# Second-layer expert dispatch: a table of slots and a gather per tile, or whole rows scattered into expert order; and the order of the start-up loads

## The chip, the cores and the metric

The kernel runs on one core of one Trainium2 chip. The metric is device time in microseconds (us) of one execution. Only the device time counts; the transposes of weights and context that the launch code makes on the host are outside it, and the change leaves them as they are.

## The reference

Two layers follow each other on x of 32 batches x 100 tokens x 256 (3200 tokens). Each layer is a cross-attention on a context of 361 rows x 192 per batch, then a mixture of experts:

```python
x = x + tanh(g_xattn[0]) * L0_xattn(layernorm(x), ctx, ...)      # 8 heads of 64
x = x + tanh(g_ffn[0])   * L0_ffn(layernorm(x), ...)             # 8 experts, top 2, hidden 512
x = x + tanh(g_xattn[1]) * L1_xattn(ctx, layernorm(x), mask, ...) # 4 heads, masked, rms-normed q and k
x = x + tanh(g_ffn[1])   * L1_ffn(layernorm(x), ...)             # 16 experts, top 4 of 2 groups, hidden 256

# L1_ffn, per expert e (we is the token's weight for e, 0 if not chosen)
h = silu(x2 @ W1[e].T + b1[e]) * (x2 @ W3[e].T + b3[e])
y = y + (h @ W2[e].T + b2[e]) * we[:, None]
```

Four of sixteen experts for each of 3200 tokens are 12,800 rows in the second expert layer.

## The kernel before

`build` (line 61) runs five stages one after the other, each a block in which the five engines have their own instruction lists and meet at a barrier at its end: `setup` (141), `attention0` (270), `experts` for layer 0 (1379), `attention1` (782), `experts` for layer 1.

**setup.** GpSimd (POOL) makes constants. SyncE's queue (SP) issues all small and middle weights of both layers, ten small vectors first, then the key and value weights of layer 0, then the others (185 to 202), and all of them are waited for (203, 212, 234). ScalarE's queue (ACT) fills two slot tables in DRAM with "empty" entries and zeroes spare rows (228 to 233). attention0 begins when all of it has landed.

**Attention, both layers.** One iteration of a software pipeline works on one batch in several phases at once: `i` is the batch whose scores are made, `i+1` to `i+4` are batches whose inputs are loaded, normalised and projected, `i-1` and `i-2` are routed. In layer 1, per iteration, SP loads x (859) and context and mask (868 to 870; line 866 waits until POOL has used the mask of two batches before), and stores x1 and the normalised rows xm (877, 879). VectorE (DVE) begins with the context's statistics (1133), which wait for that load; then come the norms, the route (1207 to 1256) and the dispatch (1263 to 1274). POOL does the roots (1312, 1336), the softmax's normalising (1349), the mask (1328), and four indirect DMAs (1357). `y_dispatch` gives each token and choice a position: the count of the expert's tokens so far, in that expert's region of the table. Each of the four DMAs of a batch writes 100 entries of 8 bytes (token number, weight) to table1 at these positions; the normalised rows go to xn1 in token order by the plain store 879.

**Experts.** The tiles have 128 rows each: 57 tiles for layer 0 and 115 for layer 1, some of them empty at the end. First DVE turns the counts into a plan (1481 to 1501): for each tile its expert (`tile_e`), its first table row (`tile_r`) and whether it is the first of its expert (`tile_s`). TensorE (PE) turns the plan into rows (1687 to 1689). Layer 1 meanwhile loads the biases, copied to all partitions (1607 to 1609, 2 MB each); DVE's first tile waits for them. Then for each tile j: SP loads 128 table entries (1570), POOL gathers the 128 rows of xn that they name (1438), PE transposes (1634), ACT copies (1583), PE multiplies by W1 and W3 (1652), DVE adds the bias (1526), ACT takes SiLU (1594), DVE multiplies (1531), PE transposes (1668), ACT copies (1600), PE multiplies by W2 (1680), DVE adds the bias (1540) and multiplies by the entry's weight (1545), POOL adds the rows to the output in DRAM by an indirect DMA (1451). POOL's list is written out: gather j+3, then scatter j-2. A scatter waits for the scatter two before it, and, where its tile is the first of an expert, for the one before it.

```python
for j in range(NT):
    gather(j + LOOK)          # xg<-xn,slots  L1438
    if j >= 2:
        scatter(j - 2)        # out<-y,slots  L1451
```

PE's list for one tile is x_transpose(j+1), down(j-2), h_transpose(j-1), up(j+1).

Of the kernel before, what the change touches and what calls it, by code (L numbers as in the profile page):

```python
# [7 lines left out]
F32 = mybir.dt.float32  # L8
# [23 lines left out]
REGION = TOKENS  # L32
# [28 lines left out]
def build(nc, a, out):  # L61
    top = ExitStack()
    dram = {}
    for n, e, t in ((0, E0, NT0), (1, E1, NT1)):
        rows = e * REGION + (t + 3) * P
        dram[f"table{n}"] = nc.dram_tensor(f"table{n}", (rows, 2), I32, kind="Internal").ap()
        dram[f"xn{n}"] = nc.dram_tensor(f"xn{n}", (TOKENS + SPARE, D), F32, kind="Internal").ap()
# [15 lines left out]
    with top:  # L83
# [12 lines left out]
            experts0_loaded=sem("experts0_loaded"), experts1_loaded=sem("experts1_loaded"),  # L96
        )
        c["wk0"] = c["expert_w"][:, 0:2 * I0].rearrange("p (k n) -> p k n", k=2)
        c["wv0"] = c["expert_w"][:, 2 * I0:4 * I0].rearrange("p (k n) -> p k n", k=2)
        first = ExitStack()  # L100
# [8 lines left out]
        experts(nc, maker, a, dram, c, 1)  # L109
# [11 lines left out]
W0_LOADS, W1_LOADS = 2 * E0, 3 * E1  # L121

# [17 lines left out]

def setup(nc, maker, a, dram, c):
    stack = ExitStack()
    with stack:
        sb, ps, sem = maker(stack)
        empty = sb("empty_slots", [P, SPARE, 2], I32)
        zero = sb("zero_rows", [P, D])
        odd, even = sb("odd", [P, 1], I32), sb("even", [P, 1], I32)
        ones_set, tables_set = sem("ones_set"), sem("tables_set")
        w_loaded, filled = sem("w_loaded"), sem("filled")
        halved, gates_done, scale_done = sem("halved"), sem("gates_done"), sem("scale_done")  # L150
        tall = (("wk0", "L0_xattn_Wk"), ("wv0", "L0_xattn_Wv"))
        small = (("wq0", "L0_xattn_Wq", P), ("wo0", "L0_xattn_Wo", P), ("wr0", "L0_ffn_moe_router", P),
                 ("wq1", "L1_xattn_WqT", P), ("wkv1", "L1_xattn_WkvT", CK), ("wlkv1", "L1_xattn_WlkvT", P),
                 ("wo1", "L1_xattn_WoT", P), ("wr1", "L1_ffn_WgT", P))
        W_LOADS = 6 + 4 + 3 * len(tall) + len(small) + 2
        FILLS = 0
        for n in range(2):
            FILLS += -(-(dram[f"table{n}"].shape[0] // SPARE) // P) + 4
        with nc.Block() as block:

            @block.gpsimd
            def _(g):
                g.memset(c["ident"][:, :], 0.0)
                g.memset(empty[:, :, :], 0)
                g.memset(zero[:, :], 0.0)
                g.memset(c["upto"][:, :, :], 1.0)
                g.memset(c["ones"][:, :], 1.0).then_inc(ones_set, 1)
                g.wait_ge(ones_set, 1)
# [3 lines left out]
                                base=0, pattern=[[1, N]], channel_multiplier=-1)  # L172
                g.affine_select(out=c["upto"][:, :, :], in_=c["upto"][:, :, :], compare_op=ALU.is_ge, fill=0.0,
# [5 lines left out]
                g.iota(c["token"][:, :], [[1, 1]], base=0, channel_multiplier=1)  # L179
                g.iota(empty[:, :, 0], [[1, SPARE]], base=TOKENS, channel_multiplier=0).then_inc(tables_set, 1)  # L180

            @block.sync
            def _(s):
                with nc.allow_non_contiguous_dma(reason="a few per-partition constants"):
                    s.dma_start(c["gates"][:, 0:2], a["g_xattn"].partition_broadcast(P)).then_inc(w_loaded, 16)
                    s.dma_start(c["gates"][:, 2:4], a["g_ffn"].partition_broadcast(P)).then_inc(w_loaded, 16)
                    s.dma_start(c["cx_g"][:, :], a["L1_xattn_ln_x_g"].rearrange("(k p) -> p k", p=CK)).then_inc(w_loaded, 16)
                    s.dma_start(c["cx_b"][:, :], a["L1_xattn_ln_x_b"].rearrange("(k p) -> p k", p=CK)).then_inc(w_loaded, 16)
                    s.dma_start(c["lt_g"][:, :], a["L1_xattn_ln_l_g"].rearrange("(k p) -> p k", p=P)).then_inc(w_loaded, 16)
                    s.dma_start(c["lt_b"][:, :], a["L1_xattn_ln_l_b"].rearrange("(k p) -> p k", p=P)).then_inc(w_loaded, 16)  # L190
                    for half in range(2):
                        r = slice(half * DH, (half + 1) * DH)
                        s.dma_start(c["qk_g"][r, 0:1], a["L1_xattn_qn_g"].rearrange("(p k) -> p k", k=1)).then_inc(w_loaded, 16)
                        s.dma_start(c["qk_g"][r, 1:2], a["L1_xattn_kn_g"].rearrange("(p k) -> p k", k=1)).then_inc(w_loaded, 16)
                for n, src in tall:
                    s.dma_start(c[n][:, 0, :], a[src][0:P]).then_inc(w_loaded, 16)
                    s.dma_start(c[n][0:CR, 1, :], a[src][P:C]).then_inc(w_loaded, 16)
                    s.dma_start(c[n][P - CR:P, 1, :], a[src][P:C]).then_inc(w_loaded, 16)
                for n, src, p in small:
                    s.dma_start(c[n][:, :, :], a[src].rearrange("(k p) n -> p k n", p=p)).then_inc(w_loaded, 16)  # L200
                s.dma_start(c["bo0"][:, :], a["L0_xattn_bo"].partition_broadcast(N)).then_inc(w_loaded, 16)
                s.dma_start(c["bo1"][:, :], a["L1_xattn_bo"].partition_broadcast(N)).then_inc(w_loaded, 16)
                s.wait_ge(w_loaded, 16 * W_LOADS)

            @block.vector
            def _(v):
                v.memset(c["neghalf"][:, :], -0.5)
                v.wait_ge(tables_set, 1)
                v.tensor_scalar(even[:, :], odd[:, :], 1, 4, ALU.arith_shift_right, ALU.logical_shift_left).then_inc(halved, 1)
                v.wait_ge(halved, 1)  # L210
                v.tensor_scalar(c["landed"][:, :], even[:, :], float(-16 * (P // 2)), None, ALU.add)
                v.wait_ge(w_loaded, 16 * W_LOADS)
                v.tensor_tensor(c["qk_s"][:, :], c["qk_g"][:, 0:1], c["qk_g"][:, 1:2], ALU.mult).then_inc(scale_done, 1)
                v.wait_ge(scale_done, 1)
                v.tensor_scalar(c["qk_s"][:, :], c["qk_s"][:, :], DH ** -0.5, None, ALU.mult)
                v.wait_ge(gates_done, 1)
                v.tensor_scalar(c["bo0"][:, :], c["bo0"][:, :], c["tg"][0:N, 0:1], None, ALU.mult)
                v.tensor_scalar(c["bo1"][:, :], c["bo1"][:, :], c["tg"][0:N, 1:2], None, ALU.mult)

            @block.scalar  # L220
            def _(s):
                s.wait_ge(tables_set, 1)
                for n in range(2):
                    t = dram[f"table{n}"]
                    assert t.shape[0] % SPARE == 0
                    blocks = t.shape[0] // SPARE
                    full = t.rearrange("(b r) c -> b (r c)", r=SPARE)
                    for at in range(0, blocks, P):
                        m = min(P, blocks - at)
                        s.dma_start(full[at:at + m], empty[0:m].rearrange("p r c -> p (r c)")).then_inc(filled, 16)  # L230
                    for at in range(TOKENS, TOKENS + SPARE, P):
                        s.dma_start(dram[f"xn{n}"][at:at + P], zero[:, :]).then_inc(filled, 16)
                        s.dma_start(dram[f"acc{n}"][at:at + P], zero[:, :]).then_inc(filled, 16)
                s.wait_ge(w_loaded, 16 * W_LOADS)
                s.activation(c["tg"][:, :], c["gates"][:, :], ACT.Tanh).then_inc(gates_done, 1)
                s.wait_ge(filled, 16 * FILLS)
# [33 lines left out]
def attention0(nc, maker, a, dram, c):  # L270
# [8 lines left out]
    with stack:  # L279
# [21 lines left out]
        x1_out, xm_out, slots_out = sem("x1_out0"), sem("xm_out0"), sem("slots_out0")  # L301
        ready, w_high, w_low = sem("ready0"), sem("w_high"), sem("w_low")
        ln_dve, ln_pool, xb_done = sem("ln_dve0"), sem("ln_pool0"), sem("xb_done0")
# [16 lines left out]
        with nc.Block() as block:  # L320

            @block.sync
            def _(s):
# [17 lines left out]
                def store(b):  # L341
                    if b >= 1:
                        s.wait_ge(x1_out, 16 * b)
                        s.wait_ge(xm_out, 16 * b)
                    s.wait_ge(x1_done, b + 1)
                    s.dma_start(acc_b[b], r["x1"][:, b % 2, :]).then_inc(x1_out, 16)
                    s.wait_ge(ln1_dve, nth(LN, b, "done"))
                    s.dma_start(xn_b[b], r["xm"][:, b % 2, :]).then_inc(xm_out, 16)

                s.wait_ge(ready, 1)  # L350
                for b in range(3):
                    load_x(b)
                    load_c(b)
                for b in range(B):
# [6 lines left out]
                    if b == B - 4:  # L361
                        load_experts0(s, a, c)
                store(B - 1)
                s.wait_ge(x1_out, 16 * B)
                s.wait_ge(xm_out, 16 * B)

            @block.tensor
# [1377 lines left out]
```

## Time and profile before

| | us |
|---|---|
| median of 3 runs (2165.41 to 2174.96) | 2169.73 |
| the profiled execution, own time | 2168.25 |
| its span, first to last instruction | 2166.5 |
| PE busy | 1943.0 (90%) |
| DVE busy | 1341.7 (62%) |
| POOL busy | 1272.2 (59%) |
| ACT busy | 926.0 (43%) |

The stages lie in the span about so: setup 0 to 26, attention0 26 to 740, experts of layer 0 740 to 1080, attention1 1090 to 1729, experts of layer 1 1729 to 2166. A timeline row has start, duration, engine, line, operation, written tile and read tiles, and in brackets how long the engine was idle before it and what ended that. A group row has count, busy time in all and mean ns of one, then the idle time before its instructions.

### The profile page before, as it was taken

The numbers are of one execution on the slowest core, as the hardware profiler recorded it, in microseconds if no ns is written. First come the engines' busy times: TensorE is split into PE (matmuls) and PEld (weight loads), VectorE is DVE, ScalarE is ACT, GpSimd is POOL, SyncE is SP. The second block draws the span as 40 slices with busy tenths as digits, with TensorE's granted clock in tenths as the row PEclk, the third lists the DMA queues.
The fourth block names the chain that finished last, engine by engine and source line by source line (L and its number), as shares of the span: only waits on it lengthen the run. The fifth ranks groups of instructions, "written<-read, shape, count | busy, mean of one in ns | idle before, by whom it ended". The sixth has DMA issues, their size and how long they took to land. (4 is left out here: it accounts for less than half of the span.)

```text
span 2166.5 us, 40335 instructions
## 1 busy us (share of the span) xinstructions
PE 1943.0 (90%) x11418; PEld 1339.4 (62%) x11418; DVE 1341.7 (62%) x4049; ACT 926.0 (43%) x2321; POOL 1272.2 (59%) x1490
## 2 busy tenths in 40 slices
PE   3999999999999289999679999999999469899997
PEld 2777777777777168888535555555555335555554
DVE  3677777777776532222348888888888435555554
ACT  1444443444433323333147666666776123333332
POOL 1344444444444344545347888888888347777776
PEclk9999999999999689999879999999999589999999
DMA  4111101011116023333211111111117154445454
GB/s 130 35 28 37 39 27 39 26 39 37 28 57 223 10 40 53 51 54 50 42 35 36 36 36 36 36 36 35 36 35 236 40 146 76 76 75 79 74 77 73
DMA packets 143799, 127.49 MB, mean 59 GB/s; under 512 B 48505, under 2 KB 134241, under 8 KB 143590
## 3 DMA queue, kind: packets, MB, share of 16 engines
q0 software_dynamic: 39456, 46.11, 13.2%
q1 hardware_dynamic: 96348, 70.67, 11.7%
q10 hardware_dynamic: 7786, 8.14, 1.1%
q8 instruction: 105, 1.72, 0.4%
q14 instruction: 104, 0.85, 0.1%
HBM read 87.16 MB, written 37.65 MB: 58 GB/s over the span
## 5 line engine op out<-in xcount | busy, mean ns | idle before, releaser
L747 POOL TENSOR_SCALAR prob<-prob,rc 100x363 f32<-100x363 f32 x256 | 158.2, 627 | 343.3 <-DVE rc L610 343.3
L1680 PE MATMUL psD<-expert_w,hT 128*128 x916 | 232.7, 387 | 3.0 <-ACT hT L1600 3.0
L1438 POOL DMA_INDIRECT xg<-xn,slots x178 | 178.9, 1005 | 91.9 <-issue 46.9
L1451 POOL DMA_INDIRECT out<-y,slots x115 | 186.5, 1621 | 75.2 <-issue 28.4
L1652 PE MATMUL psG<-expert_w,xgT 128*128 x460 | 219.7, 600 | 1.3 <-ACT xgT L1583 1.3
L937 PE MATMUL psJ<-wkv,cTn 96*121 96x512 f32 x384 | 177.7, 600 | 0.0
L1680 PEld LDWEIGHTS psD<-expert_w,hT 128*128 128x128 f32 x916 | 161.5, 191 | 21.6 <-issue 5.0
L1451 POOL DMA_INDIRECT acc<-y,slots x57 | 89.7, 1573 | 137.2 <-DVE y L1545 132.3
L536 ACT ACTIVATE prob<-psS,nm 100x361 f32<-100x361 f32 x256 | 141.5, 561 | 54.0 <-DVE nm L605 50.9
L605 DVE TENSOR_REDUCE nm<-psS 100x2 f32<-100x722 f32 x128 | 115.0, 898 | 71.6 <-PE psS L434 71.4
L1357 POOL DMA_INDIRECT table<-slot,pos x128 | 137.7, 1076 | 35.6 <-issue 30.1
L1583 ACT ACTIVATE xgT<-psX 128x256 f32<-128x256 f32 x115 | 44.1, 383 | 256.1 <-PE psX L1634 256.1
L1522 DVE TENSOR_TENSOR hid<-psU,gate 128x512 f32<-128x512 f32 x57 | 39.4, 691 | 159.1 <-PE psU L1642 159.1
L1634 PEld LDWEIGHTS psX<-ident,xg 128*128 128x128 f32 x344 | 41.6, 142 | 151.8 <-DMA xg<-xn,slots 104.2
L1600 ACT ACTIVATE hT<-psH 128x256 f32<-128x256 f32 (+1 forms) x172 | 77.8, 452 | 129.6 <-PE psH L1668 127.3
L1336 POOL TENSOR_TENSOR rk<-rk,neghalf 121x12 f32<-121x12 f32 x64 | 126.9, 1982 | 5.3
L1526 DVE TENSOR_TENSOR pre<-psG,bias 128x512 f32<-128x512 f32 x115 | 79.5, 691 | 76.1 <-PE psG L1652 68.8
L614 DVE COPY pT<-psT 121x600 f32<-121x600 f32 x128 | 99.1, 774 | 42.8 <-PE psT L442 42.7
L1634 PE MATMUL psX<-ident,xg 128*128 128x128 f32 x344 | 71.0, 288 | 60.7 <-DMA xg<-xn,slots 45.3
L541 ACT ACTIVATE oT<-psO 128x100 f32<-128x100 f32 x128 | 32.4, 253 | 206.4 <-PE psO L455 202.7
L1060 ACT ACTIVATE kv<-psJ 121x512 f32<-121x512 f32 (+2 forms) x160 | 88.0, 550 | 69.7 <-PE psJ L937 69.7
L1652 PEld LDWEIGHTS psG<-expert_w,xgT 128*128 128x128 f32 x460 | 79.7, 194 | 58.3 <-issue 58.3
(271 smaller groups left out, 5049.6 us busy)
## 6 DMA issues: line engine op xcount, KB each, us to landing
expert_w<-in_L_ffn_moe_w SPq DMA_DIRECT2D x8, 1024.0 KB, 13.6
xn<-xm SPq DMA_DIRECT2D x64, 100.0 KB
bias<-in_L_ffn_b ACTq DMA_DIRECT2D x3, 2048.0 KB, 13.8
ctx<-in_ctx SPq DMA_DIRECT2D x32, 181.5 KB
cT<-in_ctxT SPq DMA_DIRECT2D x32, 180.5 KB
cT<-in_ctxT SPq DMA_DIRECT2D x64, 90.2 KB
expert_w<-in_L_ffn_moe_w SPq DMA_DIRECT2D x8, 512.0 KB, 12.3
expert_w<-in_L_ffn_W1T SPq DMA_DIRECT2D x16, 256.0 KB
```

Source lines behind the costliest of these rows:

```text
L536: s.activation(prob[:, q, 0:S], psS[0:N, h, 0:S], ACT.Exp, bias=nm[:, q:q + 1], accum_out=rs[:, q:q + 1]).then_inc(exp_done, 1)
L605: v.tensor_reduce(nm[:, q2:q2 + 2], psS[0:N, :, 0:S], AX, ALU.max, negate=True).then_inc(max_done, 1)
L614: v.tensor_copy(pT[:, p % 2, :, :, :], psT[0:CH, :, 0:NCH * N].rearrange("p h (j n) -> p h j n", j=NCH)).then_inc(t_out, 1)
L747: g.tensor_scalar(prob[:, q, :], prob[:, q, :], rc[:, q:q + 1], 1.0, ALU.mult, ALU.mult).then_inc(prob_done, 1)
L937: mm = t.matmul(ph[0:rows, 0:cols], lhs, wt[:, k, :], start=k == 0, stop=k == 1)
L1336: g.tensor_tensor(rk[:, b % 3, lo:hi, :], rk[:, b % 3, lo:hi, :], neghalf[0:CH, 0:1].unsqueeze(2).to_broadcast([CH, hi - lo, H1]), ALU.pow ...
L1357: g.indirect_dma_start(table, bass.IndirectOffsetOnAxis(r["pos"][:, b % 2, k:k + 1], 0), r["slot"][:, b % 2, k, :], None).then_inc(slots_o ...
L1438: g.indirect_dma_start(xg[:, j % 4, :], None, xn_rows, bass.IndirectOffsetOnAxis(slots[:, j % RING, 0:1].bitcast(U32), 0)).then_inc(gather ...
L1451: g.indirect_dma_start(acc, bass.IndirectOffsetOnAxis(slots[:, j % RING, 0:1].bitcast(U32), 0), y[:, j % 4, :], None, compute_op=ALU.add). ...
L1634: mm = t.transpose(psX[:, k * P:(k + 1) * P], xg[:, j % 4, k * P:(k + 1) * P], ident[:, :])
L1652: mm = t.matmul(psG[:, r, :], xT[:, r, k, :], w13[:, bass.ds(e, 1), k, 0:512], start=k == 0, stop=k == 1)
L1680: mm = t.matmul(psD[:, r, 0:D], hT[:, r, k, :], w2[:, bass.ds(e, 1), k, :], start=k == 0, stop=k == KF - 1)
```

## The change

It touches the start of the kernel and the second layer's way from attention to experts.

- **Start.** setup no longer waits for weights: SP loads only the key and value weights of layer 0, ACT the six other loads that attention0 needs; the fills and the 14 loads for attention1 are issued by SP within attention0, between the inputs of batch 1 and those of batch 2. Waits for each group stand where it is first used: TensorE and ACT for layer 0's weights, POOL's first slot scatter for the fills, DVE at iteration 8 for layer 1's weights.
- **Row scatter.** table1 and xn1 are gone. attention1 keeps for each token one row of 273 floats (256 normalised values, the token number, the 16 expert weights, zero where not chosen) and scatters the whole row (1092 bytes) four times, to the position in each chosen expert's region of `rows1`. The store of xm is gone. DVE's wait for these scatters moves from the dispatch to the norm and looks two batches further back.
- **Plan.** The 18 small DVE steps, the PE rows and the three copies stand at the end of attention1's lists. SP and ACT each end 8 regions with 128 empty rows (DRAM to DRAM, 16 copies of 140 KB) once the counts are known; the stage ends when they have landed.
- **Experts of layer 1** are a function of their own: SP loads tile j's 128 rows with one plain DMA into a ring of 8; there is no table load and no gather, POOL only scatters. The weight is a column of the row, picked by the tile's expert number.

```diff
-REGION = TOKENS
+REGION = TOKENS + P
+ROW = D + 1 + 16
...
+            @block.sync        # setup
+                for n, src in (("wk0", "L0_xattn_Wk"), ("wv0", "L0_xattn_Wv")):
+                    s.dma_start(c[n][:, 0, :], a[src][0:P]).then_inc(c["kv0_loaded"], 16)
...
-                s.wait_ge(w_loaded, 16 * W_LOADS)
...
                 # attention0, sync
-                s.wait_ge(ready, 1)
-                for b in range(3):
+                for b in range(2):
                     load_x(b)
+                    if b == 0:
+                        s.wait_ge(ready, 1)
                     load_c(b)
+                fill(s, dram, c)
+                load_attention1(nc, s, a, c)
+                load_x(2)
+                load_c(2)
...
                 # attention1, sync, store(b)
-                    s.dma_start(acc_b[b], r["x1"][:, b % 2, :]).then_inc(x1_out, 16)
-                    s.wait_ge(ln1_dve, nth(LN, b, "done"))
-                    s.dma_start(xn_b[b], r["xm"][:, b % 2, :]).then_inc(xm_out, 16)
+                    s.dma_start(acc_b[b], r["x1"][:, b % 2, :]).then_inc(stored, 16)
...
                 # attention1, vector
                 def y_norm(b):
+                    if b >= 4:
+                        v.wait_ge(slots_out[b % 2], 64 * (b // 2 - 1))
-                    v.tensor_scalar(r["xm"][:, b % 2, :], r["x1"][:, b % 2, :], ...
+                    v.tensor_scalar(row[:, b % 4, 0:D], r["x1"][:, b % 2, :], ...
                 def route_weights(b):
-                    n = rt.inc(v.tensor_scalar(w, top_v[:, 0:TOP1], tmp[:, 1:2], ROUTE_SCALE, ALU.mult, ALU.mult))
+                    n = rt.inc(v.scalar_tensor_tensor(w, r["sc"][:, 0, :], tmp[:, 1:2], r["chosen"][:, :], ALU.mult, ALU.mult))
...
                 # attention1, gpsimd, scatter(b, k)
-                    g.indirect_dma_start(table, bass.IndirectOffsetOnAxis(r["pos"][:, b % 2, k:k + 1], 0),
-                                         r["slot"][:, b % 2, k, :], None).then_inc(slots_out[b % 2], 16)
+                    g.indirect_dma_start(rows, bass.IndirectOffsetOnAxis(pos[:, b % 4, k:k + 1], 0),
+                                         row[:, b % 4, :], None).then_inc(slots_out[b % 2], 16)
...
+        def empty_tails(engine, which):
+            for e in which:
+                end = engine.value_load(base_i[0:1, e:e + 1], ...)
+                engine.dma_start(rows[bass.ds(end, P), :], rows[E1 * REGION:E1 * REGION + P, :]).then_inc(emptied, 16)
...
+def experts1(nc, maker, a, dram, c):
+            @block.sync
+                for j in range(NT):
+                    if j >= RING:      # RING = 8
+                        s.wait_ge(scattered[j % 2], 16 * ((j - RING) // 2 + 1))
+                    if j >= 4:
+                        s.wait_ge(rows_in[j % 4], 16 * (j // 4))
+                    at_row = s.value_load(tile_r[0:1, j:j + 1], ...)
+                    s.dma_start(xr[:, j % RING, :], rows[bass.ds(at_row, P), :]).then_inc(rows_in[j % 4], 16)
+            @block.gpsimd
+                for j in range(NT):
+                    scatter(j)
+            @block.vector      # weighted(j)
+                    v.tensor_scalar(y[:, j % 4, :], yb[:, j % 2, :], row_w[:, j % RING, bass.ds(e, 1)], None, ALU.mult)
```

The lists of TensorE, ACT and the rest of DVE in experts1 are those of layer 1 before.

## Rows read from the trace of the kernel before

**Rows 1.** Windows: the tiles of experts layer 1, and attention1; busy us (instructions) by engine, clock, DMA share, GB/s

```profile
1754.20:2153.40 399.20, 366.32 (x1360) 208.96 (x1360) 217.37 (x453) 130.72 (x342) 290.74 (x223) 0.99 0.48 74
1154.00:1690.00 536.00, 519.57 (x3158) 312.62 (x3157) 440.38 (x1732) 365.33 (x810) 454.31 (x570) 0.99 0.20 57
```

**Rows 2.** Groups by line and shape, and waits, in 1770 to 2150 us

```profile
L1451 POOL DMA_INDIRECT out<-y,slots x108 | 175.4, 1624 | 64.6 <-issue 27.1 <-DVE y L1545 16.5 <-DMA out<-y,slots 15.5
L1438 POOL DMA_INDIRECT xg<-xn,slots x109 | 107.6, 987 | 33.2 <-issue 27.7 <-PE psX L1634 2.7 <-DVE y L1545 2.1
...
PE psX L1634 <- DMA xg<-xn,slots: 31.1, 30, 2.5
```

**Rows 3.** Timeline of PE and DVE around 1930 us; line 1545, ns min/median/max

```profile
1922.53 1.88 PE L1652 MATMUL psG<-expert_w,xgT 128*128 x4
1925.55 1.88 PE L1652 MATMUL psG<-expert_w,xgT 128*128 x4
...
1935.71 0.69 DVE L1526 TENSOR_TENSOR pre<-psG,bias 128x512 f32<-128x512 f32 x1 [0.18 <-issue]
...
1938.87 0.69 DVE L1526 TENSOR_TENSOR pre<-psG,bias 128x512 f32<-128x512 f32 x1
...
L1545 DVE TENSOR_SCALAR y<-yb,slots x108: 352/353/610, 1771.6 to 2149.1; 128x256 f32<-128x256 f32 x108
```

**Rows 4.** One round of attention1 in the timelines of POOL, SP's queue and DVE

```profile
1416.66 1.01 POOL L1328 TENSOR_SCALAR mb<-m 100x361 f32<-100x361 uint8 x1
...
1418.49 0.31 SPq L870 DMA_DIRECT2D m<-in_mask  x1
...
1421.34 0.88 DVE L1133 BATCH_NORM_STATS2 cst<-ctx 121x6 f32<-121x192 f32 x3 [0.96 <-DMA m<-in_mask]
...
1422.66 0.26 POOL L1310 TENSOR_SCALAR crs<-cmv 121x3 f32<-121x3 f32 x1 [0.41 <-DVE cmv L1137]
...
1434.82 1.01 POOL L1328 TENSOR_SCALAR mb<-m 100x361 f32<-100x361 uint8 x1
```

**Rows 5.** Line 1357 in 1250 to 1600 us, and landing of table scatters and of row gathers

```profile
L1357 POOL DMA_INDIRECT table<-slot,pos x76: 987/1082/1124, 1251.2 to 1593.0; - x76
DMA to landing us min/median/max: 2.1/2.2/4.4
...
DMA to landing us min/median/max: 2.7/2.8/6.1
```

**Rows 6.** Timeline and windows of the start

```profile
11.00:14.00 3.00, 0.00 (x0) 0.00 (x0) 0.00 (x0) 1.28 (x1) 0.00 (x0) 1.00 1.07 383
...
25.25 0.16 DVE L213 TENSOR_TENSOR qk_s<-qk_g 128x1 f32<-128x1 f32 x1 [20.73 <-DMA bo<-in_L_xattn_bo]
...
33.69 0.64 PE L397 MATMUL psJ<-c_hi,wk_hi 128*128 128x362 f32 x1 [33.69 <-DVE c_hi L590]
...
48.76 0.82 ACT L528 ACTIVATE c_hi<-cT 128x728 fp32r<-128x728 f32 x1
...
50.41 0.56 ACT L536 ACTIVATE prob<-psS,nm 100x361 f32<-100x361 f32 x1 [0.28 <-DVE nm L605]
```

**Rows 7.** From attention1 to the experts: timeline, SP's pace, landing of the three bias loads

```profile
1718.81 0.23 DVE L1256 TENSOR_SCALAR slot<-slot,tg 100x4 f32<-100x4 f32 x1
...
1723.76 0.99 POOL L1357 DMA_INDIRECT table<-slot,pos  x1 [0.30 <-issue]
1729.42 0.40 ACTq L1607 DMA_DIRECT2D bias<-in_L_ffn_b  x1
...
1736.59 0.38 SPq L1570 DMA_DIRECT2D slots<-table  x1
...
1737.75 1.51 SPq L1570 DMA_DIRECT2D slots<-table  x2
...
1754.19 0.69 DVE L1526 TENSOR_TENSOR pre<-psG,bias 128x512 f32<-128x512 f32 x1 [18.55 <-PE psG L1652]
...
DMA to landing us min/median/max: 8.0/13.8/19.9
```

More of the change, by code:

```diff
@@ L138, in load_experts1, with fill @@
         s.dma_start(w2[:, e], a["L1_ffn_W2T"][e].rearrange("(k p) d -> p k d", p=P)).then_inc(loaded, 16)
+ATTENTION0 = (("wq0", "L0_xattn_Wq"), ("wo0", "L0_xattn_Wo"), ("wr0", "L0_ffn_moe_router"))
+ATTENTION1 = (("wq1", "L1_xattn_WqT", P), ("wkv1", "L1_xattn_WkvT", CK), ("wlkv1", "L1_xattn_WlkvT", P),
+              ("wo1", "L1_xattn_WoT", P), ("wr1", "L1_ffn_WgT", P))
+KV0_LOADS, W0_LOADED, W1_LOADED = 3, 3 + len(ATTENTION0), 4 + 4 + len(ATTENTION1) + 1
+def fill(s, dram, c):
+    filled = c["filled"]
+    t = dram["table0"]
+    assert t.shape[0] % SPARE == 0
+    blocks = t.shape[0] // SPARE
+    full = t.rearrange("(b r) c -> b (r c)", r=SPARE)
+    for block in range(0, blocks, P):
+        m = min(P, blocks - block)
+        s.dma_start(full[block:block + m], c["empty"][0:m].rearrange("p r c -> p (r c)")).then_inc(filled, 16)
+    for row in range(TOKENS, TOKENS + SPARE, P):
+        for n in ("xn0", "acc0", "acc1"):
+            s.dma_start(dram[n][row:row + P], c["zero"]).then_inc(filled, 16)
+    trailing = dram["rows1"][E1 * REGION:].rearrange("(t two p) c -> p t two c", two=2, p=P)
+    for two in range(2):
+        s.dma_start(trailing[:, :, two, :], c["empty_rows"][:, two, :].unsqueeze(1).to_broadcast([P, TRAILING // 2, ROW])).then_inc(filled, 16)
@@ new lines, in fills, with load_attention1 @@
+def fills(dram):
+    return -(-(dram["table0"].shape[0] // SPARE) // P) + 6 + 2
+def load_attention1(nc, s, a, c):
+    loaded = c["w1_loaded"]
+    with nc.allow_non_contiguous_dma(reason="a few per-partition constants"):
+        s.dma_start(c["cx_g"][:, :], a["L1_xattn_ln_x_g"].rearrange("(k p) -> p k", p=CK)).then_inc(loaded, 16)
+        s.dma_start(c["cx_b"][:, :], a["L1_xattn_ln_x_b"].rearrange("(k p) -> p k", p=CK)).then_inc(loaded, 16)
+        s.dma_start(c["lt_g"][:, :], a["L1_xattn_ln_l_g"].rearrange("(k p) -> p k", p=P)).then_inc(loaded, 16)
+        s.dma_start(c["lt_b"][:, :], a["L1_xattn_ln_l_b"].rearrange("(k p) -> p k", p=P)).then_inc(loaded, 16)
+        for half in range(2):
+            r = slice(half * DH, (half + 1) * DH)
+            s.dma_start(c["qk_g"][r, 0:1], a["L1_xattn_qn_g"].rearrange("(p k) -> p k", k=1)).then_inc(loaded, 16)
+            s.dma_start(c["qk_g"][r, 1:2], a["L1_xattn_kn_g"].rearrange("(p k) -> p k", k=1)).then_inc(loaded, 16)
+    for n, src, p in ATTENTION1:
+        s.dma_start(c[n][:, :, :], a[src].rearrange("(k p) n -> p k n", p=p)).then_inc(loaded, 16)
+    s.dma_start(c["bo1"][:, :], a["L1_xattn_bo"].partition_broadcast(N)).then_inc(loaded, 16)
@@ L179, in _ @@
                 g.iota(c["token"][:, :], [[1, 1]], base=0, channel_multiplier=1)
+                g.wait_ge(ones_set, 4)
+                for two in range(2):
+                    g.iota(c["empty_rows"][:, two, D:D + 1].bitcast(I32), [[1, 1]], base=TOKENS + two * P, channel_multiplier=1)
                 g.iota(empty[:, :, 0], [[1, SPARE]], base=TOKENS, channel_multiplier=0).then_inc(tables_set, 1)
@@ L183, in _ @@
             def _(s):
[L184 to L202, printed above, removed]
-                s.wait_ge(w_loaded, 16 * W_LOADS)
+                for n, src in (("wk0", "L0_xattn_Wk"), ("wv0", "L0_xattn_Wv")):
+                    s.dma_start(c[n][:, 0, :], a[src][0:P]).then_inc(c["kv0_loaded"], 16)
+                    s.dma_start(c[n][0:CR, 1, :], a[src][P:C]).then_inc(c["kv0_loaded"], 16)
+                    s.dma_start(c[n][P - CR:P, 1, :], a[src][P:C]).then_inc(c["kv0_loaded"], 16)
             @block.vector
@@ L213, in _ @@
[L213 to L218, printed above, removed]
@@ L220, in _ @@
             @block.scalar
             def _(s):
[L222 to L233, printed above, removed]
@@ L887, in _ @@
                         load_experts1(s, a, c)
-                s.wait_ge(x1_out, 16 * B)
-                s.wait_ge(xm_out, 16 * B)
+                s.wait_ge(plan, 1)
+                empty_tails(s, range(0, E1 // 2))
+                s.wait_ge(stored, 16 * B)
+                s.wait_ge(emptied, 16 * E1)
             @block.tensor
@@ L1038, in _ @@
                     at(i + 3, lat_transpose)
+                t.wait_ge(plan, PLANNED)
+                t.matmul(psY[0:1, 2 * P:3 * P], tf[:, 5:6], ident[:, :], start=True, stop=True)
+                t.matmul(psY[0:1, 0:P], tf[:, 2:3], ident[:, :], start=True, stop=True)
+                t.matmul(psY[0:1, P:2 * P], tf[:, 3:4], ident[:, :], start=True, stop=True).then_inc(plan, 1)
             @block.scalar
@@ L1124, in _ @@
                     at(i, p_transposed, 1)
+                s.wait_ge(plan, 1)
+                empty_tails(s, range(E1 // 2, E1))
             @block.vector
```

344 lines of the change are left out of this document (266 added, 78 removed).

## The prediction

> **What bounds the kernel now.** I read the page first, then windows over each stage, since PE is busy 90% on average and that says nothing of the places this change touches. In the tiles of the last stage PE is busy 366 of 399 us; in attention1 520 of 536 [rows 1]. The groups and waits of the last stage [rows 2] and one stretch of its timeline [rows 3] then say why PE isn't full, and the timeline of attention1 [rows 4] what sets its pace. Start and hand-over are chains of few steps, read off the timeline [rows 6, 7].
>
> **Last stage.** Its tiles take 399.2 / 114 = 3.50 us each, from the first bias addition to the last [rows 1]. Where nothing holds PE up, two tiles' first products start 3.02 us apart [rows 3]: that is PE's own work. POOL's own work for a tile is 1.62 (scatter) + 0.99 (gather), and 27.1 + 27.7 us of "issue" over 108 tiles, 0.51: 3.12 us, before it waits for anything [rows 2]. So POOL, not PE, is the narrowest engine, and its waits for landings and for y come on top; PE pays as a wait for gathered rows (31.1 us as a matmul's wait, 0.29 us a tile, the rest as weights that come late) [rows 2].
>
> The change takes the gather (0.99 + 0.3) off POOL, which then needs at most 1.62 + 0.5 = 2.1 us. SP's plain load of a tile runs up to eight tiles ahead, and costs SP 1.16 us per issue with its register read (two starts, 1736.59 and 1737.75) [rows 7]: hidden. Next in line are PE at 3.02 and DVE. From one `pre` to the next (1935.71, 1938.87) DVE took 3.16 us with hardly a pause that wasn't its own, and with a y multiplication at its longest, 0.61 us [rows 3]. That operation takes 0.35 us in the median [rows 3]; so DVE needs 2.90, and some 0.1 more, as y now takes its factor from a column chosen by a register. Both engines thus stand at 3.0 and each waits for the other once per tile. I take 3.10; the ends are 3.02 (PE's floor) and 3.25. Gain: (3.50 - 3.10) x 114 = 46 us; ends 55 and 28.
>
> The spread of y, 0.35 to 0.61 us [rows 3], is what decides between DVE and PE. The Trainium skill (GPSIMD Engine Reference, Specifications) says that GpSimd shares its SBUF interfaces with VectorE, with contention for VectorE's instructions in a 2-port mode or with two SBUF inputs. By it y would be fast in nearly all tiles once the gathers are gone, which speaks for the end of 3.02 us, where the gain is 55 us.
>
> **Start.** attention0 can't begin until the last bias vector has landed, 25.25 us; PE starts at 33.69 [rows 6]. After the change only 1 MB of key and value weights and 1.1 MB on ACT's queue stand ahead; the loads ran at 383 GB/s once the queues were full [rows 6], so with a first issue at 1 us they have landed at about 9.5 us. Splitting the key weights (1.9 us), x and context of batch 0 behind them, and the split of the context bring PE's first product to about 13.3: 20.4 us sooner. But SP now issues 10 fills and 14 loads (24 x about 0.6 us, 5 MB, 14 to 15 us at the same rate) ahead of batch 2's context, which lands at about 31.5. ACT converts it at 48.76 [rows 6], which would be 28.4 now; ACT's list is in order, so it stands 3.1 us, and its next softmax step, at 50.41, had 0.8 us to spare behind the conversion's end at 49.58: 2.3 us of the gain go. Start: -18 us; ends -21 and -14 (loads slower, a second stall at batch 3).
>
> **attention1.** POOL sets the pace, with a loop through a load: POOL ends a mask (1416.66 + 1.01), SP may load the next context and mask (issued 1418.49), DVE begins statistics at 1421.34, POOL takes up their result at 1422.66 and is at the next mask at 1434.82: 18.16 us a round, of which POOL waits only 0.41 [rows 4]. What the change removes here (the store of xm, DVE's near wait for slots) lies beside this loop and brings nothing: DVE doesn't stand at the dispatch. What it adds: the four scatters write 437 KB a round where they wrote 3 KB. POOL's own time for one was 1.07 us for 100 rows of 8 bytes [rows 5] and 0.99 for 128 rows of 1 KB [rows 2], so it goes by rows, not bytes, and I leave it. But one of the four is issued right beside the mask's load, on the same DMA engines. The nearest rows: 8-byte scatters land after 2.2 us, 1 KB gathers after 2.8 [rows 5]. Ends 0 and 0.6 us a round; 109 KB at 383 GB/s is 0.3, which I take: POOL then waits that much longer in some 30 rounds, +9 us; ends 0 and +18.
>
> The Trainium skill (DMA: Bandwidth & Descriptors, section "Queues, rings and completion order") says against the change that each DMA engine takes its queues in turn, a whole packet at a time. With that page's fit ("Anatomy of one DMA") of 2.0 us plus bytes over 436 GB/s, an estimate is 0.25 us for each scatter, +7.5 us where I have +9.
>
> **Hand-over.** The plan (the first table load follows it 7.2 us after the block's start at 1729.42) moves from 1718.8 + 0.2 on, where DVE has ended its last route step, under POOL's last scatters, which end at 1724.75 [rows 7]. It looks like 7 us gained and a gather on top, but the experts' first tile needs the biases, too: three loads issued from 1729.42, the last of which takes 19.9 us to land from about 1731.6 [rows 7], hence 22.1 us after the block's start. DVE's first addition was at 1754.19, 24.8 us after it. So at most 2.7 us are to be had, less 2 for the eight row loads (1.1 MB) beside the biases. And the block starts later: 8 copies on each of SP and ACT at 1.16 us each from about 1719.4 (route's end, plus the first plan step) end at 1728.7, landing 2.5 or more later, barrier: about 1732.8 for 1729.42. +3.4 +2 -2.7, and 1.7 back because the second tile's product is ready by then: +1 us; ends -3 and +7.
>
> **Sum** against the profiled execution (span 2166.5, own time 2168.25): -18 + 9 - 46 + 1 = -54, so 2114; its own time lies 1.5 us below the median of the runs, 2169.7, which is nothing. The plan in attention1's tail, the DVE route steps (as many as before) and the twice-as-wide weights cost nothing: they stand beside POOL's scatters.
>
> **The rivals.**
> A. The last stage doesn't come down to PE's pace, since DVE's loop of 2.9 to 3.0 us beats against PE's, or scatter-adds in turn (1.62 us and a landing of some 3) hold the y ring: 3.25 us a tile, -28 instead of -46: 2132. For: DVE's 3.16 with no pause [rows 3]. Against: the stretched y came from POOL work half of which goes.
> B. The mask's load isn't delayed, as the rows of the scatter flow before or after it, and PE runs at its floor: -20 - 55 + 0 = -75, less 1: 2093. For: DMA share in attention1 is only 0.20 [rows 1].
> C. The full 0.6 us a round, or more (1.0): +18 to +30: 2123 to 2135.
> D. Slower than before: POOL's descriptor time for a wide scatter is that of the scatter-add, 1.62 instead of 1.07 us, as both write rows of 1 KB to DRAM. Four times in 31 rounds of a POOL-bound loop this is +68 us: 2182. It decides from (54 + 11) / 124 = 0.52 us more per scatter on. For: the only write of wide rows in the trace takes 1.62. Against: that one adds in DRAM; width alone cost the gather nothing.
> E. The change doesn't reach the last stage: the row loads come as late as the gathers did (SP waits for scatters eight tiles back). 3.50 a tile remain: 2160. Against: eight tiles are 28 us.
>
> **How the numbers follow.** Forecast 0.48, A 0.19, B 0.12, C 0.10, D 0.07, E 0.04. The predicted time is the forecast's, 2114. The range takes in B and the slow ends of A and C: 2092 to 2142, which leaves out D, E and the far tails, some 2 in 10. No change is within 0.5%, 2159 to 2181, about what a measurement of this kernel can tell. E lies at its edge and half of D inside it: faster 0.90, same 0.05, slower 0.05.
>
> **What the profile of the changed kernel would show.** PE's first product near 13 us, and ACT idle before the conversion of batch 2's context for some 3 us. In attention1 1.0 to 1.1 us per POOL scatter, rounds of 18.2 to 18.7 us, and DVE's wait for the mask up from 0.96 to about 1.3. The first bias addition of the last stage 22 to 24 us after its block starts, released by the bias load and no longer by PE. Then 3.10 us a tile, no wait of PE for a row load, POOL busy about half. I am wrong if POOL's scatter takes over 1.3 us, if the round passes 18.9 us, or if a tile takes over 3.25.

## The result, and the profile after

| | before | after |
|---|---|---|
| median of six runs each | 2167.16 us (2164.23 to 2174.96) | 2150.36 us (2146.92 to 2154.43) |
| profiled execution, span | 2166.5 | 2150.0 |
| PE / DVE / POOL busy | 1943.0 / 1341.7 / 1272.2 | 1955.2 / 1348.4 / 1147.7 |

The ratio is 0.9925, with a 95% interval of [0.9911, 0.9939]: faster, as forecast, but by less than 1%: 17 us instead of 54, and outside the range of 2092 to 2142. Split at marks, the spans differ as follows; the last column is what the prediction gave, and the first row is a part of the second.

| stretch | before | after | difference | predicted |
|---|---|---|---|---|
| PE's first product | 33.69 | 18.48 | -15.2 | -20.4 |
| up to the last scatter of attention1 | 1723.76 | 1719.14 | -4.6 | -18 + 9 |
| from there to the first `pre` | 30.4 | 32.8 | +2.3 | +1 |
| 114 tiles, first to last `pre` | 399.2 | 382.9 | -16.3 | -46 |
| last `pre` to the end | 13.1 | 15.2 | +2.1 | 0 |

So 30 of the missing 37 us are in the tiles. The start came out 13 short, attention1 9 better than feared, and the last two stretches took 3 more than I gave.

Windows of the kernel after, for the tiles and for attention1, in the columns of [rows 1]:

```profile
1751.92:2134.81 382.89, 370.81 (x1356) 214.10 (x1356) 215.35 (x452) 120.54 (x340) 171.68 (x111) 0.99 0.49 78
1154.00:1690.00 536.00, 517.77 (x3127) 311.91 (x3126) 448.41 (x1727) 363.16 (x807) 452.89 (x572) 0.98 0.25 74
```

POOL's busy time in the tiles fell from 290.74 to 171.68 us, and still a tile takes 382.89 / 114 = 3.36 us. What stands in the way shows in the groups of 1770 to 2080 us (line, engine, shapes, count | busy, mean ns | idle before it and what ended it):

```profile
L1826 POOL DMA_INDIRECT out<-y,xr x93 | 143.8, 1546 | 171.1 <-DMA out<-y,xr 85.1 <-DVE y L1857 77.9 <-issue 8.1
L1842 DVE TENSOR_TENSOR pre<-psG,bias 128x512 f32<-128x512 f32 x92 | 63.7, 692 | 44.2 <-issue 44.0
L1847 DVE TENSOR_TENSOR hid<-pre,gate 128x256 f32<-128x256 f32 x92 | 39.2, 426 | 44.3 <-ACT gate L1889 44.3
L1852 DVE TENSOR_TENSOR yb<-psD,bias 128x256 f32<-128x256 f32 x92 | 39.1, 425 | 33.5 <-issue 33.5
L1889 ACT ACTIVATE gate<-pre 128x256 f32<-128x256 f32 x92 | 38.3, 416 | 201.1 <-DVE pre L1842 201.1
```

POOL waits 171 us here, so it no longer sets the pace. ACT waits 201 us for DVE's `pre`. And DVE, for which everything waits, stands still before `pre` for 44.0 / 92 = 0.48 us a tile and before `yb` for 0.36, for nothing that the profile shows ("issue"). DVE's timeline over one tile says where:

```profile
1922.91 0.69 DVE L1842 TENSOR_TENSOR pre<-psG,bias 128x512 f32<-128x512 f32 x1 [0.44 <-issue]
1924.09 0.43 DVE L1847 TENSOR_TENSOR hid<-pre,gate 128x256 f32<-128x256 f32 x1 [0.48 <-ACT gate L1889]
1924.86 0.42 DVE L1852 TENSOR_TENSOR yb<-psD,bias 128x256 f32<-128x256 f32 x1 [0.35 <-issue]
1925.43 0.35 DVE L1857 TENSOR_SCALAR y<-yb,xr 128x256 f32<-128x256 f32 x1
1926.21 0.69 DVE L1842 TENSOR_TENSOR pre<-psG,bias 128x512 f32<-128x512 f32 x1 [0.42 <-issue]
```

Ahead of `pre` and of `yb` the program calls `expert(j)`, which reads the tile's expert out of SBUF into a register. The engine has nothing to execute until the number is there. The page's chain of work that ended last, which in the kernel before had DMA, PE and POOL ahead of DVE, now has DVE first and DVE's own sequencer (DVEq) second:

```profile
DVE 8%; DVEq 3%; DMA 3%; issue 3%; ACT 2%; PE 0%; POOLq 0%; ACTq 0%; POOL 0%
```

**The theories.** V: the register reads in DVE's list pace the tiles of the kernel after. Its rivals, L and S in the expectations, put the pace of 3.36 us elsewhere than in DVE's reads, so that taking one away would bring little or nothing (2143 us or more). For the kernel before, the question is whether GpSimd's two indirect DMAs set the pace, so that DVE's reads cost it nothing. W and C are theories of the start, H and R of the hand-over.

### The profile page after: what moved, and what is told of

Same layout as the page of the kernel before. It is cut to its first block and busy times, and to the rows that moved or that the text cites. A ratio compares the mean times of both kernels' runs of the same rounds, so it can differ in the third digit from the quotient of the medians.

```text
span 2150.0 us, 40169 instructions
## 1 busy us (share of the span) xinstructions
PE 1955.2 (91%) x11418; PEld 1350.0 (63%) x11418; DVE 1348.4 (63%) x4050; ACT 917.3 (43%) x2321; POOL 1147.7 (53%) x1375
## 5 line engine op out<-in xcount | busy, mean ns | idle before, releaser
L1826 POOL DMA_INDIRECT out<-y,xr x115 | 177.9, 1547 | 246.9 <-DVE y L1857 131.6
L1432 POOL DMA_INDIRECT rows<-row,pos_of x128 | 137.8, 1077 | 35.6 <-issue 30.1
L1889 ACT ACTIVATE gate<-pre 128x256 f32<-128x256 f32 x115 | 47.9, 416 | 249.6 <-DVE pre L1842 249.6
L1941 PE MATMUL psD<-expert_w,hT 128*128 x460 | 128.9, 402 | 12.6 <-ACT hT L1895 8.1
L465 PEld LDWEIGHTS psT<-ident,prob 100*121 100x121 f32 x768 | 95.2, 187 | 27.8 <-POOL prob L779 20.4
L457 PE MATMUL psS<-kT,qT 64*100 64x361 f32 x512 | 110.9, 506 | 0.7 <-ACT prob L558 0.7
L465 PE MATMUL psT<-ident,prob 100*121 100x100 f32 x768 | 109.1, 278 | 2.4 <-POOL prob L779 2.4
L544 ACT ACTIVATE kT<-psJ 128x361 f32<-128x361 f32 x128 | 60.9, 476 | 115.8 <-PE psJ L420 115.8
L1754 PE MATMUL psD<-expert_w,hT 128*128 x456 | 108.1, 380 | 1.6 <-ACT hT L1674 1.6
## 6 DMA issues: line engine op xcount, KB each, us to landing
bias<-in_L_ffn_b ACTq DMA_DIRECT2D x3, 2048.0 KB, 15.9
```

The costliest lines, as they stand in the source:

```text
L457: t.matmul(psS[0:N, h, 0:S], qT[rows, b % 2, p, :], kT[rows, b % 2, p, :], start=True, stop=True).then_inc(s_mm, 1)
L465: mm = t.transpose(psT[0:CH, h, j * N:(j + 1) * N], prob[:, (2 * p + h) % 4, j * CH:(j + 1) * CH], ident[0:N, 0:N])
L1432: g.indirect_dma_start(rows, bass.IndirectOffsetOnAxis(pos[:, b % 4, k:k + 1], 0), row[:, b % 4, :], None).then_inc(slots_out[b % 2], 16)
L1826: g.indirect_dma_start(acc, bass.IndirectOffsetOnAxis(row_token[:, j % RING, :], 0), y[:, j % 4, :], None, compute_op=ALU.add).then_inc(sc ...
L1941: mm = t.matmul(psD[:, r, 0:D], hT[:, r, k, :], w2[:, bass.ds(e, 1), k, :], start=k == 0, stop=k == KF - 1)
```

## The experiments

Each ran beside the kernel before on the same chip; ratios are to it, with 95% intervals. The four kernels of the first group share one series of runs of before (2165.6 us), the four of the second another (2165.74). The kernel changed as in the diff is called "after"; its own 0.9925 comes from the series of the result, so a difference to it is one of two ratios.

**One register read a tile, in after.** The expert of tile j + 1 is read while DVE would wait for the gate anyway; `weighted` takes up the register that `hidden` used.

```diff
-                    r, e = j % 2, expert(j)
+                    r, e = j % 2, experts_of[j]
...
                     v.tensor_tensor(pre ...).then_inc(pre_done, 1)
+                    if j + 1 < NT:
+                        load_expert(j + 1)
                     v.wait_ge(g_out, j + 1)
...
-                    e = expert(j)
+                    e = experts_of.pop(j)
```

> The changed kernel with one edit in the last stage: VectorE reads each tile's expert number into a register once instead of twice, and does so between its bias addition and its wait for SiLU, where it stands idle anyway. Theory V (VectorE's own list is the bound, with the two register reads of 0.34 and 0.45 us in it): the tile falls from 3.36 us to between 3.02 (TensorE's own work) and 3.12, 114 tiles give 27 to 39 us, time 2111 to 2123 us. Theory L (the landing of the scatter-adds, for which GpSimd waits 97 us over 108 tiles, holds the pace) or theory S (ScalarE's order, SiLU ahead of the copy that TensorE needs, holds it): 3.3 us a tile or more stay, time 2143 us or more.

Measured 2109.86 us (2108.81 to 2110.50), ratio 0.9743 [0.9725, 0.9760]: V, and just below its bounds. DVE's timeline and the window of the tiles:

```profile
1925.19 0.69 DVE L1844 TENSOR_TENSOR pre<-psG,bias 128x512 f32<-128x512 f32 x1 [0.59 <-PE psG L1929]
1926.36 0.42 DVE L1851 TENSOR_TENSOR hid<-pre,gate 128x256 f32<-128x256 f32 x1 [0.48 <-PE psH L1937]
1926.70 0.42 DVE L1856 TENSOR_TENSOR yb<-psD,bias 128x256 f32<-128x256 f32 x1
1927.27 0.43 DVE L1861 TENSOR_SCALAR y<-yb,xr 128x256 f32<-128x256 f32 x1
1928.21 0.69 DVE L1844 TENSOR_TENSOR pre<-psG,bias 128x512 f32<-128x512 f32 x1 [0.51 <-PE psG L1929]
...
1749.44:2094.40 344.96, 343.31 (x1352) 211.28 (x1353) 205.13 (x453) 134.10 (x340) 172.52 (x111) 0.99 0.54 87
```

Now DVE waits for PE, 0.5 to 0.6 us a tile, and PE is busy 343.31 of 344.96 us. The pace is 3.03 us, the 3.02 of [rows 3]. L and S are dead: the landings of the scatter-adds and ACT's order are what they were, and the pace is PE's. The rows also give the price of a read: from `hid` to `yb` it is 0.34 us from start to start here (1926.36 to 1926.70), and 0.77 with the read between them in after (1924.09 to 1924.86).

**A third read, in after.** One more `expert(j)` ahead of `pre`, its result unused.

```diff
                 def hidden(j):
+                    expert(j)
                     r, e = j % 2, expert(j)
```

> The changed kernel with one more, unused, register read of the expert number per tile on VectorE, ahead of the one for the bias addition. Theory V: each read costs its whole length, 0.35 to 0.7 us a tile, so 40 to 80 us more, 2190 to 2230 us. Theories L and S: VectorE has slack, the read hides, less than 10 us more.

Measured 2220.60 us (2217.32 to 2224.11), ratio 1.0257 [1.0234, 1.0280]. That is V again, inside its 2190 to 2230, and one operation with no output makes the kernel 2.6% slower than before the change. In the groups of the same stretch the idle time before `pre` is now 84.5 / 78 = 1.08 us where it was 0.48:

```profile
L1843 DVE TENSOR_TENSOR pre<-psG,bias 128x512 f32<-128x512 f32 x78 | 53.9, 691 | 84.5 <-issue 84.5
```

The extra 0.60 us a tile are the whole price: from first to last `pre` it takes 450.95 us, 68.1 more, or 0.60 x 114. The added time is paid in full, as it must be if DVE's list is the bound.

**One read a tile, in the kernel before.** The same edit there, where the gathers are still on GpSimd.

```diff
-                        e = v.value_load(tile_e[0:1, j:j + 1], min_val=0, max_val=E - 1)
+                        e = experts_of[j]
...
+                        if j + 1 < NT:
+                            load_expert(j + 1)
```

> The kernel before, with the same edit to VectorE's register reads as in the run with one read. If GpSimd's gather and scatter were the bound there, as the prediction had it (3.12 us of own work plus waits, 3.50 a tile), nothing is to be had: 0 to -6 us, 2161 to 2168 us. If VectorE's list was already the bound in most tiles and the gathers only came late now and then, then the reads give most of what they give after the change: -15 us or more, 2152 us or less.

Measured 2164.27 us (2160.22 to 2168.24), ratio 0.9991 [0.9977, 1.0005]: no difference that can be measured, as a pace set by GpSimd would have it. Its groups in 1770 to 2080 us:

```profile
L1451 POOL DMA_INDIRECT out<-y,slots x90 | 145.6, 1618 | 49.9 <-issue 22.0 <-DVE y L1552 15.7 <-DMA out<-y,slots 11.9
L1438 POOL DMA_INDIRECT xg<-xn,slots x90 | 88.8, 986 | 27.5 <-issue 25.3 <-PE psX L1641 0.9 <-DMA slots<-table 0.7
```

They add up to 311.8 us for 90 tiles, 3.46 each, of which POOL waits for anything only 30. DVE, with its read gone, waits for PE's product ahead of `pre` instead (116.3 us in 114 tiles). That POOL's list, and not the landing of the gathers, held PE back before is read off these sums; no kernel had the one without the other. In the one profiled execution the tiles are faster (391.9 for 399.2 us), so a few us may be in it. The four kernels together are the clearest reading of this case: one read fewer alone gives 0.9991, the change alone 0.9925, both together 0.9743, and the 114 tiles take 399.2 us before, 391.9 and 382.9 with the one or the other, 345.0 with both. Two limits at nearly the same height hide from each other what the removal of either is worth.

**The old start, in after.** Loads and fills are issued and waited for within setup again, though with the key and value weights at their head; the rest is after.

```diff
+                load_attention1(nc, s, a, c)
+                s.wait_ge(c["kv0_loaded"], 16 * 2 * KV0_LOADS)
+                s.wait_ge(c["w1_loaded"], 16 * W1_LOADED)
...
+                fill(s, dram, c)
...
-                fill(s, dram, c)
-                load_attention1(nc, s, a, c)
```

> The changed kernel with the start undone: all loads and fills are issued within setup and waited for at its end, nothing stands ahead of batch 2's context. The traces say that the new start brings TensorE's first product 15.2 us forward and gives back about 11 of them at batch 2's context, so undoing it costs 4 to 5 us: 2154 to 2156 us. If the rest of the 11 us is lost for another reason (the clock, a slower first batch), the undone start is worth as little or less; if it costs 15 or more, the gain wasn't given back.

Measured 2157.28 us (2154.90 to 2159.66), ratio 0.9963 [0.9949, 0.9977], just above the 2154 to 2156 expected; so the whole new start is worth 0.0038, 8 us. It's a little more than the 4.6 us of the marks, since here PE's first product is at 36.20, later than before's 33.69. Where did the 15 us go that PE begins sooner?

**Batch 2's loads first, in after.** SP issues them ahead of layer 1's weights instead of behind them.

```diff
                 fill(s, dram, c)
-                load_attention1(nc, s, a, c)
                 load_x(2)
                 load_c(2)
+                load_attention1(nc, s, a, c)
```

> The changed kernel with one move in SyncE's list of the first attention: the loads of batch 2's x and context are issued ahead of the second layer's attention weights, not behind them. In the changed kernel's trace ScalarE stands still for 6.71 us at 40.41 for that context. Theory W (the start's lead of 15.2 us at TensorE's first product shrinks to 4.3 at the plan partly by this wait): the wait goes, and the whole comes out 4 to 7 us under the changed kernel's 2150.4 us, at 2143 to 2146.5. Theory C (the lead is lost because the first 100 us are bound by the granted clock and by VectorE's own work, and the wait lies beside that): within 1.5 us, 2149 to 2152.

Measured 2140.87 us (2138.41 to 2145.19), ratio 0.9884 [0.9864, 0.9903]. Against after's 0.9925 that is 0.0041, 9 us: theory C is dead, and it is more than theory W's 4 to 7. In the profiled executions the last scatter of attention1 even comes 13.4 us sooner (1705.76), but of these two after's was 1.4 us slower than its median and this one 2.5 us faster. First the wait itself. SP's queue and ACT in after:

```profile
20.46 1.15 SPq L170 DMA_DIRECT2D rows<-expert_w  x2
21.66 1.44 SPq L180 DMA_DIRECT2D cx_g<-in_L_xattn_ln_x_g  x1
23.14 1.26 SPq L181 DMA_DIRECT2D cx_b<-in_L_xattn_ln_x_b  x1
24.45 1.26 SPq L182 DMA_DIRECT2D lt_g<-in_L_xattn_ln_l_g  x1
25.76 1.28 SPq L183 DMA_DIRECT2D lt_b<-in_L_xattn_ln_l_b  x1
...
33.35 0.36 SPq L352 DMA_DIRECT2D cT<-in_ctxT  x1
...
40.41 0.81 ACT L550 ACTIVATE c_hi<-cT 128x728 fp32r<-128x728 f32 x1 [6.71 <-DMA cT<-in_ctxT]
```

SP needs until 33.35 us to reach batch 2's context, and ACT can convert it only 7 us after that, while the DMA engines still move what was issued ahead of it (busy share 0.84 from 35 to 40 us). ACT stands 6.71 us where I had 3.1. The four issues of 1.26 to 1.44 us aren't slow because they load small vectors: in the kernel of this experiment it is batch 2's context that stands in that place behind the fills and is issued slowly, and the vectors behind it aren't.

```profile
24.81 1.16 SPq L352 DMA_DIRECT2D cT<-in_ctxT  x1
...
29.14 0.45 SPq L182 DMA_DIRECT2D lt_g<-in_L_xattn_ln_l_g  x1
```

Then PE's clock. Windows of 5 us from 35 us on, first of after, then of this kernel (PE, PEld, DVE, ACT, POOL, granted clock, DMA share, GB/s):

```profile
35.00:40.00 5.00, 0.41 (x3) 0.11 (x1) 0.26 (x2) 0.00 (x0) 1.16 (x2) 0.96 0.84 220
40.00:45.00 5.00, 3.42 (x16) 3.45 (x17) 1.07 (x2) 2.48 (x7) 0.00 (x0) 0.50 0.02 3
45.00:50.00 5.00, 4.71 (x22) 3.24 (x23) 3.08 (x7) 0.00 (x0) 2.21 (x5) 0.50 0.00 2
50.00:55.00 5.00, 5.00 (x36) 3.89 (x36) 1.70 (x4) 1.87 (x7) 1.06 (x3) 0.68 0.33 94
```

```profile
35.00:40.00 5.00, 4.04 (x33) 3.34 (x31) 4.17 (x10) 1.58 (x6) 2.61 (x4) 1.00 0.90 261
40.00:45.00 5.00, 5.00 (x44) 3.49 (x43) 2.22 (x5) 2.07 (x7) 2.72 (x6) 1.00 0.36 100
45.00:50.00 5.00, 5.00 (x29) 3.67 (x29) 3.40 (x6) 1.20 (x4) 0.85 (x2) 1.00 0.00 0
```

In after PE sits idle for 6.2 us (35.4 to 41.6), and the granted clock of the next two windows is 0.50, the lower of its two levels (1.2 GHz), and 0.68 in the one behind them. Without the wait it stays at 1.00, and the fourth conversion of a context, at 63.3 us in after, starts at 52.7: 10.6 us sooner, 3.9 more than the wait. It is 34.1 us behind PE's first product here as in the kernel before (18.58 to 52.70, 33.69 to 67.80), so the start's lead of 15 us is now kept whole. That the 3.9 us are the clock's is argued from the windows; no kernel had the one without the other.

**The third bias load on its own semaphore, in after.** The first addition needs b1 and b3; b2 is needed at the first `yb`.

```diff
-                v.wait_ge(bias_in, 16 * 3)
+                v.wait_ge(bias_in, 16 * 2)
...
+                    if j == 0:
+                        v.wait_ge(bias_in2, 16)
```

> The changed kernel, with its bias loads on two semaphores: the first VectorE addition of the second experts waits for the first two of the three bias loads only, and the third is waited for ahead of the first use of its table. The three land at 9.3, 15.9 and 19.3 us after the first issue, and the first addition ends its wait with the last of them. Theory H (hand-over: that third load is the last thing the block waits for): 3 to 7 us under the changed kernel's 2150.4, at 2143 to 2147. Theory R (the first row tiles and TensorE's first products end the wait just as late, 16 us into the block): within 1.5 us.

Measured 2145.24 us (2143.09 to 2150.67), ratio 0.9904 [0.9883, 0.9925]. The medians' ratio says 4.5 us less than after, inside theory H's 3 to 7, though the two intervals overlap. The profile is plainer: from the last scatter to the first `pre` it is 27.4 us for 32.8, 5.4 less.

```profile
1745.65 0.69 DVE L1843 TENSOR_TENSOR pre<-psG,bias 128x512 f32<-128x512 f32 x1 [25.80 <-PE psG L1927]
```

PE had that product ready at 1742.0, so the wait more likely ended with the second bias load, whatever the row names: the three were issued from 1728.3 to 1731.1 and landed after 9.4, 15.9 and 18.9 us.

**The wait for the empty tails' copies later, in after.**

```diff
-                s.wait_ge(emptied, 16 * E1)
...
             # experts1, sync, ahead of the first row load
+                s.wait_ge(c["emptied"], 16 * E1)
```

> The changed kernel, with the wait for the 16 copies that fill the empty tail of the row table moved from the end of the second attention to the point in the experts' own list just ahead of the first row load, so that the block and its bias loads begin without them. The last scatter is at 1719.1 and the bias loads are issued at 1729.2, 10.0 us later, against 5.7 in the kernel before. Theory H (the copies' wait delays the bias loads, and these end the hand-over): 2 to 4 us under 2150.4, at 2146.5 to 2148.5. If the row loads, still behind the copies, end the hand-over: within 1.5 us.

Measured 2148.07 us (2146.71 to 2152.01), ratio 0.9913 [0.9894, 0.9933]. Undecided: 2.6 us less by the ratios, within the intervals, and 0.9 us less from scatter to `pre` (31.8). The biases are issued at 1728.04 instead of 1729.16 only: ACT and SP issue their eight copies each until 1725.1, 6 us after the last scatter's start, and the barrier comes 2.9 us later. The issue of the copies rather than their landing would then be the greater part of the delay; no kernel had them issued elsewhere.

**All four together.** The one register read and the last three edits.

> The changed kernel with one register load for a tile in VectorE's list, together with the three edits of the other kernels of this call (batch 2's loads first, two bias semaphores, late wait for the empty copies). If the hand-over and the start are paid in full and add to the tiles' gain: the 2109.9 us of the kernel with one register load, less 9 to 16, so 2094 to 2101. If only the tiles count and the others lie beside other waits: 2107 to 2111.

Measured 2092.03 us (2089.05 to 2096.28), ratio 0.9657 [0.9635, 0.9679], the fastest of all, 74 us under before and 2 under the 2094 to 2101 expected. Against the kernel with one read it is 18.6 us less in the span: 9.9 up to the last scatter, 7.1 from there to the first `pre`, and 1.6 in the tiles, where PE is now busy all the time:

```profile
1732.43:2075.81 343.38, 343.25 (x1357) 211.08 (x1356) 204.86 (x452) 133.87 (x340) 171.95 (x111) 1.00 0.57 93
```

## Why the prediction was wrong

**The step that failed.** It is this one, of the last stage: "That operation takes 0.35 us in the median [rows 3]; so DVE needs 2.90, and some 0.1 more". The loop of 3.16 us [rows 3] had a y of 0.61 us, and I took 0.26 off for a short one. But beneath y's execution ran the register read for the next tile. The trace of before has loops with a short y that show it, and I hadn't looked at them:

```profile
1769.20 0.69 DVE L1526 TENSOR_TENSOR pre<-psG,bias 128x512 f32<-128x512 f32 x1 [0.29 <-issue]
...
1771.15 0.42 DVE L1540 TENSOR_TENSOR yb<-psD,bias 128x256 f32<-128x256 f32 x1 [0.35 <-issue]
1771.61 0.35 DVE L1545 TENSOR_SCALAR y<-yb,slots 128x256 f32<-128x256 f32 x1
1772.36 0.69 DVE L1526 TENSOR_TENSOR pre<-psG,bias 128x512 f32<-128x512 f32 x1 [0.39 <-issue]
...
1938.12 0.61 DVE L1545 TENSOR_SCALAR y<-yb,slots 128x256 f32<-128x256 f32 x1
```

This loop takes the same 3.16 us (1769.20 to 1772.36), and `pre` follows y's start after 0.75 us behind the short y (1771.61) as behind the long one (1938.12, with `pre` at 1938.87). A shorter y only uncovers the read. The right sum was 3.16 for the loop as it stood, plus 0.11 for y's new factor, a column chosen by a register: from `yb` to y it is 0.46 us from start to start in the rows above, and 0.57 in after (1924.86 to 1925.43). That makes 3.27, which the fastest tiles of after take; the one shown takes 3.30 and the average is 3.36, since `pre` follows y's start after 0.76 to 1.24 us there, and why that varies is open. Against the 3.10 that I took the step cost 30 us in 114 tiles, and the prediction's own sign of being wrong, a tile over 3.25 us, is there. The timeline of before shows such idle time as "issue" in front of `pre` [rows 3]; I had read it as a small gap of the engine's own instead of as an instruction that can be counted and priced.

Rival A named the right engine and not the mechanism: it kept the loop of 2.9 to 3.0 us and let it beat against PE's, where DVE's loop alone is longer than PE's. Its 3.25 us was still too low, and with it its 2132.

The Trainium skill (GPSIMD Engine Reference, Specifications) was weighed there, for the SBUF interfaces that GpSimd shares with VectorE: with half of GpSimd's work gone, y would be fast in nearly all tiles and PE's floor would be reached. Of y the trace bears it out: it takes over 0.37 us in 24 of the 115 tiles before, and in 3 after (its row in after, min/median/max ns, is below). But what was freed went to the register read, not to the pace.

```profile
L1857 DVE TENSOR_SCALAR y<-yb,xr x115: 352/354/667, 1759.8 to 2140.4; 128x256 f32<-128x256 f32 x115
```

**Start.** Forecast -18, worth -8 by experiment and -4.6 by the marks. Its first half had the first product at 13.3 and it came at 18.48. The key and value weights were there at 12.2, not 9.5, but PE waited for the first context, which landed at 15.12; and ACT's table load, done at 11.86 while everything waited in the kernel before, now stood between it and its conversion at 16.41:

```profile
15.12 1.28 ACT L550 ACT_TABLE_LOAD   x1 [15.12 <-DMA cT<-in_ctxT]
```

Its second half named the right wait (ACT, for batch 2's context) with 3.1 us for 6.7. The 24 issues took 16.3 us (16.61 to 32.94) for 14.4, and the context then wasn't there at about 31.5, but at 40.4. That PE's idle time would be followed by some 13 us at the lower clock level wasn't in it at all.

**attention1.** Forecast +9, measured 0: from the mask conversion at 1141.30 to the one at 1669.97 it takes 528.67 us before, and between the same two after (1137.08 to 1665.51) 528.43. POOL's scatter of a whole row takes what the narrow one took [rows 5], which kills rival D, and lands 0.7 us later in the median:

```profile
L1432 POOL DMA_INDIRECT rows<-row,pos_of x76: 988/1082/1855, 1252.9 to 1595.7; - x76
...
DMA to landing us min/median/max: 2.7/2.9/5.8
```

DVE's wait for the mask's load stayed at 1 us (23.6 us in 24 waits, for 28.2 in 26 before), so the transfer beside it didn't delay it, and rival C is dead, too; of B's two halves this one held. The 7.5 us that I had estimated from the Trainium skill (DMA: Bandwidth & Descriptors, "Queues, rings and completion order"), by which the queues take turns, don't show in this loop. Whether they take turns isn't settled by it: the scatters' landing did grow, and bytes that land later matter only if someone waits for them.

**Hand-over.** +2.3 for +1. The bias loads are issued 10.0 us behind the last scatter for 5.7 before, a delay of 4.4 where I had 3.4, and from there to the first `pre` it is 22.8 us for 24.8. The third bias load, which lands after 19.3 us, is what ends it, as the split bias load shows. From the last `pre` to the end it took 2.1 us more than before, half of it ahead of the last scatter-add's start and half behind; I hadn't looked at that stretch, and no run explains it. Rival E is dead: PE waited for a row load once, at the start of the block.

## What to carry to other kernels

When the bottleneck is moved off one engine, write out the next engine's loop as start-to-start times, and count its register reads as instructions: here each cost 0.4 to 0.6 us in the engine's own list, and to drop one of the two and hide the other in a wait that was there anyway was worth more than the whole change (40 us against 17). A short operation's time can't be taken off a loop when something else runs beneath it. And at the start, put the next consumer's data ahead of bulk work in the issuing queue: a wait that lets PE fall idle can be followed by a stretch at the lower clock.

## What the runs showed that I had not expected

- A register read from SBUF ahead of a DVE instruction: 0.36 us of idle time before `yb` and 0.48 before `pre` in the mean, and 0.60 for one more in a row, in which the engine executes nothing. A part of a read can run beneath the instruction ahead of it, so the idle time is less than the read takes.
- The row scatter of GpSimd costs the same for rows of 8 bytes and of 1 KB (medians 1.08 and 1.08 us for 100 rows); the scatter-add takes 1.55 for 128.
- SP's issues of four small vectors took 1.26 to 1.44 us each right behind the fills. It goes by the place and not by what is loaded: in the kernel with batch 2's loads first the context's loads in that place took 1.16 and 1.24, and the same four vectors 0.45 to 0.61.
- After 6.2 us without work PE was granted the lower clock level (0.50 in the windows from 40 to 50 us, 0.68 in the next); before, PE began at 33.69 and had 1.00 throughout the start.
